# A four-layer transformer stack on one core: another order for the last chunks between the mixing layers and the expert layer

## The chip, the cores and the metric

The kernel runs on one core of a Trainium2 chip. The metric is the device time of one execution in microseconds (us), the median of three runs. The engines are TensorE (PE in the profile), VectorE (DVE), ScalarE (ACT), GpSimd (POOL) and SyncE (SP), which work from queues of their own and wait for one another by semaphores.

## The reference, cut to what matters

```python
x = x + layernorm(attention(layernorm(x)))                  # 32 x 256 rows of 128
x = x + layernorm(ffn(layernorm(x)))                        # gated hidden layer of 512, two gelu layers
x = x + layernorm(recurrence(layernorm(x)))                 # h = tanh(xt + h @ Wh.T + bh)
x = x + layernorm(experts(layernorm(x)))
def experts(x):
    shared_out = (silu(x @ sg) * (x @ su)) @ sd
    logits = x @ gate_w                                     # 32 experts
    expert = argmax(logits);  score = sigmoid(max(logits))
    xs = (x * score)[argsort(expert)]                       # rows sorted by expert
    routed = (silu(xs @ g[e]) * (xs @ u[e])) @ d[e]
    return shared_out + routed[inverse order]
```

All is float32 with 8192 rows of 128 numbers. The recurrence runs over the 256 positions of all 32 sequences at once. A chunk of 512 rows holds 16 positions, that is 16 steps of 32 columns, and the state goes on from chunk to chunk.

## The kernel before, in words

After an attention stage the rows go through the mixing stage in 16 chunks of 512 rows (numbers 0 to 15). Each chunk passes a pipeline of rounds: first norm and the feed-forward layers (PE lines 1371 to 1451), third norm and the recurrence, the shared part of the expert layer, routing, and a scatter of its rows into the DRAM tensor `sorted_d`, in which each expert owns pages of 128 rows. After the last full round a function called `drain` in each engine's program finishes the chunks that are still in the pipe. It is called with n2, n1, n0 = 13, 14, 15, and chunk 12 is left to scatter. Then the slot stage reads `sorted_d` in pairs of pages, runs the routed experts (PE lines 1529, 1543, 1551, 1558) and writes the output by indirect DMAs from POOL.

The change touches `drain` alone, with the helpers that it calls. Every engine executes its own list in order, so the lists are the schedule. What they hold for one chunk:

- DVE: `sums` and `residual` (line 1755, 1738, 1766), `recurrence_norm` (1738, writes `xn3`), `choose` (1782 to 1793, top expert and one-hot), `shared(q, m)` (1746, 1750, the two halves m = 0, 1 of the shared expert's hidden layer `shid`), `state_stats` (1729, 1733), `gated` (1800 to 1810, the gated row, owner and row number into `row_buf`), `third_sum` (1738, 1870, `hs` and the sum into `row_buf`, then its statistics), `third_norm` (1738, writes `xn4`), `turn_pages` (1821 to 1838, page bookkeeping, 14 small operations) and `place` (1853 to 1860, the row positions `pos_i`).
- POOL: `rstd` (1212, 1214), the root behind each norm, and `scatter` (1223), four indirect DMAs that need `pos`, `rows` and `sh_out` of their chunk.
- ACT: the tanh of each recurrence step (1578), copies out of PSUM (`recurrence_turned` 1594, `router_turned` 1590, `shared_out` 1598, `state_turned` 1608), the gate's tanh (1603) and the shared part's tanh (1584).
- PE: `turn4` (1279, transposes), `recurrence_in` (1333), `rnn` (1286, one recurrence step), `logits` (1316), `ranks` (1340 to 1345), `shared` (1311), `shared_down` (1324), `state_turn` (1356) and `keep_busy` (1351), products that nobody reads.

A recurrence step is a round trip: PE's small product adds into `xi`, ACT's tanh writes `state`, and the next product waits for it. The 16 steps of chunk 15 lie in the drain with nothing else of the pipeline beside them.

There are two row buffers: even chunks use `row_buf[0]`, odd ones `row_buf[1]`, and `third_sum` waits until the buffer's former chunk has been scattered:

```python
apply("h", hs, lambda k: hs[:, k, :], "hn", h)
wait(dve, s[f"placed{side}"], 8 * CT * (h - side))
dve.tensor_tensor(third, hs[:], old[:], ALU.add).then_inc(s["x3"], 1)
```

SP issues the loads of the experts' weights (`wgu`, `wd`, 2 MB each DMA) as soon as the last product of chunk 15's feed-forward layer is done. They run on the same 16 DMA engines as the scatters.

## Time and profile before

| | |
|---|---|
| runs | 1768.71, 1770.89, 1771.26 us; median 1770.89 |
| the profiled execution, its own time | 1770.72 us |
| its span | 1769.0 us |
| PE busy | 1650.8 us (93%) |
| DVE busy | 1317.2 us (74%) |
| ACT busy | 889.0 us (50%) |
| POOL busy | 1000.8 us (57%) |
| last product of the feed-forward layers ends | about 1492.2 us |
| first transpose of the slot stage starts | 1566.25 us |

Times in the trace count from the span's start. The drain is the stretch from about 1492 to 1566 us, and the slot stage fills the rest. Busy time of PE is counted from records whose ends are modelled, so a PE that shows as busy can still be short of its peak. The granted clock is given as a share of 2.4 GHz: 1.00 or 0.50, and a value between is a stretch that has both.

### The profile page before, as it was taken

The page shows a single profiled execution, that of the slowest core. Times are in us where ns is not written, and L with a number is a line of the kernel's source. Part 1 is how long each engine was busy: PE and PEld are TensorE (multiplying, and loading weights), DVE is VectorE, ACT ScalarE, POOL GpSimd, SP SyncE. Part 2 cuts the span into 40 slices and gives each one's busy share as a digit, 9 for nine tenths or more (in the row PEclk, how much of TensorE's full clock was granted, in tenths as well). Part 3 has the DMA queues.
Part 4 walks back from the last instruction along what each step waited for, and adds up shares of the span by engine and source line. Part 5 has one row for each costly group of instructions (what it writes and reads, how often), then busy time and mean ns, then how long its engine had stood idle before and what let it go on. Part 6 is the DMA issues. An engine that isn't in the chain of part 4 may idle for free.

```text
span 1769.0 us, 47120 instructions
## 1 busy us (share of the span) xinstructions
PE 1650.8 (93%) x14871; PEld 1237.2 (70%) x14871; DVE 1317.2 (74%) x3869; ACT 889.0 (50%) x2003; POOL 1000.8 (57%) x1782
## 2 busy tenths in 40 slices
PE   5999999999999999849999999999999999789996
PEld 3677777777777777537788888777787886555553
DVE  5588888888888888745567777777777775748886
ACT  2666666666666666514444444444444442224443
POOL 7788888888888888712223333333333333227777
PEclk9999999999999999969999999999999999689998
DMA  1011111111111113010110000000000002434441
GB/s 42 11 50 55 51 49 50 50 49 51 53 54 54 54 54 104 14 36 25 60 60 31 31 31 31 22 30 23 28 30 29 25 25 99 155 116 134 134 131 41
DMA packets 78259, 95.96 MB, mean 54 GB/s; under 512 B 7046, under 2 KB 62995, under 8 KB 78160
## 3 DMA queue, kind: packets, MB, share of 16 engines
q1 hardware_dynamic: 70992, 77.91, 13.9%
q0 software_dynamic: 7168, 16.87, 2.7%
q8 instruction: 46, 0.75, 0.2%
q14 instruction: 53, 0.43, 0.1%
HBM read 53.14 MB, written 43.69 MB: 55 GB/s over the span
## 4 chain that ended last, share of the span: by engine, by line
PE 39%; DVE 8%; issue 5%; POOL 2%; DMA 1%; ACT 1%; DVEq 0%; POOLq 0%; SPq 0%; ACTq 0%
PE main L1371 6%; PE main L1373 5%; PE main L1380 5%; PE main L1529 3%; PE yp L1451 3%; PE main L1311 2%; PE xi L1286 2%; PE main L1435 2%; PE main L1324 2%; PE main L1438 1%; PE main L1436 1%; PE route L1543 1%; PE xi L1543 1%; PE turn L1279 1%; POOL out L1269 1%
## 5 line engine op out<-in xcount | busy, mean ns | idle before, releaser
L662 ACT ACTIVATE wgu<-score 128x384 f32<-128x384 f32 x512 | 223.2, 490 | 80.2 <-PE score L484 78.8
L1371 PE MATMUL main<-hT_high,h_high 128*128 128x512 f32 x512 | 221.2, 432 | 0.9 <-ACT hT_high L1628 0.9
L1373 PE MATMUL main<-hT_high,h_low 128*128 128x512 f32 x512 | 201.3, 393 | 0.0
L506 PE MATMUL outp<-wgu 128*32 128x256 f32 (+1 forms) x4096 | 196.3, 333 | 3.3 <-POOL wgu L327 2.2
L327 POOL TENSOR_SCALAR_AFFINE_SELECT wgu<-wgu 128x512 f32<-128x512 f32 x256 | 166.4, 655 | 52.0 <-ACT wgu L662 34.3
L506 PEld LDWEIGHTS outp<-wgu 128*32 128x32 f32 x4096 | 116.6, 111 | 69.5 <-issue 23.3
L1380 PE MATMUL main<-hT_low,h_high 128*128 128x512 f32 x512 | 138.3, 391 | 0.1
L1936 DVE SCALAR_TENSOR_TENSOR th<-th,main 128x512 f32<-128x512 f32 x64 | 43.9, 685 | 115.2 <-ACT th L1655 115.2
L544 PE MATMUL back<-wout,wgu 128*128 128x128 f32 x1024 | 128.6, 280 | 0.0
L544 PEld LDWEIGHTS back<-wout,wgu 128*128 128x128 f32 x1024 | 121.8, 195 | 0.4
L1269 POOL DMA_INDIRECT out<-res,idx x96 | 96.7, 1008 | 44.3 <-issue 40.7
L1286 PEld LDWEIGHTS xi<-state,wh_sb 128*128 128x128 f32 x512 | 93.2, 195 | 38.4 <-ACT state L1578 22.3
L1578 ACT ACTIVATE state<-xi,bias 128x32 f32<-128x32 f32 x256 | 73.0, 285 | 85.5 <-PE xi L1286 83.8
L1380 PEld LDWEIGHTS main<-hT_low,h_high 128*128 128x128 f32 x512 | 96.1, 188 | 21.9 <-DVE hT_low L1890 0.8
L514 PE MATMUL total<-wgu,pick 128*32 128x256 f32 (+1 forms) x2048 | 108.2, 329 | 0.0
L1212 POOL TENSOR_SCALAR bve_f<-bmv_f 128x4 f32<-128x4 f32 x16 | 7.7, 483 | 175.9 <-DVE bmv_f L1733 175.9
L1371 PEld LDWEIGHTS main<-hT_high,h_high 128*128 128x128 f32 x512 | 97.0, 189 | 13.6 <-ACT hT_high L1628 1.4
L1619 ACT ACTIVATE hT_high<-main,sc 128x512 fp32r<-128x512 f32 x64 | 44.0, 687 | 124.1 <-PE main L1380 124.1
L1207 POOL TENSOR_TENSOR hT_low<-wgu,hT_high 128x512 fp32r<-128x512 f32 x64 | 82.7, 1292 | 41.3 <-ACT wgu L1620 41.0
L1373 PEld LDWEIGHTS main<-hT_high,h_low 128*128 128x128 f32 x512 | 97.1, 190 | 11.7 <-issue 0.2
L1529 PE MATMUL main<-wgu,xgT 128*128 x192 | 101.6, 612 | 3.4 <-DVE hid_g L1989 2.4
L680 ACT ACTIVATE wgu<-back 128x512 f32<-128x512 f32 x128 | 76.4, 597 | 51.4 <-PE back L559 48.1
(295 smaller groups left out, 4361.4 us busy)
## 6 DMA issues: line engine op xcount, KB each, us to landing
sorted_d<-row_buf SPq DMA_DIRECT2D x26, 772.0 KB, 3.7
xg<-sorted_d SPq DMA_DIRECT2D x48, 386.0 KB
wgu<-in_gate_up SPq DMA_DIRECT2D x4, 2048.0 KB
xa<-in_x SPq DMA_DIRECT2D x32, 128.0 KB, 3.4
xr<-in_x SPq DMA_DIRECT2D x32, 128.0 KB, 3.2
x_d<-x SPq DMA_DIRECT2D x32, 128.0 KB, 1.8
x1c<-x_d SPq DMA_DIRECT2D x16, 256.0 KB, 2.8
x1v<-x_d SPq DMA_DIRECT2D x16, 256.0 KB, 2.7
```

The costliest lines, as they stand in the source:

```text
L327: pool.affine_select(out=blocks, in_=blocks, compare_op=ALU.is_ge, fill=0.0, base=0, pattern=[[0, 4], [1, P]], channel_multiplier=-1).then ...
L506: m = pe.matmul(outp[AUG * j:AUG * (j + 1), p % 2, k * P:T], val[par][:, k, h, v:v + AUG], weights(h, k), start=(k == 0), stop=(k == 1), t ...
L514: m = pe.matmul(total[AUG * j:AUG * (j + 1), k * P:T], pick[:, g, :], weights(GH * g + j, k), start=(g == 0 and k == 0), stop=(g == GROUPS ...
L544: m = pe.matmul(back[:, i * P:(i + 1) * P], onT[1 - par][:, c, i * P:(i + 1) * P], wout[:, c, :], start=(c == 0 and i == 0), stop=(c == PA ...
L662: act.activation(prob[:, h // 2 % (RING // 2), :, h % 2, :], score[h % BANKS][:, 0:SC].rearrange("p (c q) -> p c q", q=P), ACT.Exp).then_i ...
L1207: pool.tensor_tensor(hT_part[1][1][:, m, :], hT[1][:, m, :], hT_part[1][0][:, m, :].bitcast(F32), ALU.subtract).then_inc(s["h2_low"], 1)
L1269: pool.indirect_dma_start(out=out_rows[:, :], out_offset=bass.IndirectOffsetOnAxis(ap=idx[k][:, n:n + 1], axis=0), in_=res[k][:, n, :], in ...
L1286: pe.matmul(xi[:, o:o + B], wh_sb[:], state[:, prev:prev + B], start=False, stop=(t == STEPS - 1), skip_group_check=True).then_inc(s["p_st ...
L1371: pe.matmul(main[m % 2][:, :], w[0][:, k, m * P:(m + 1) * P], src[0][:, k, :], start=(k == 0), stop=False)
L1373: pe.matmul(main[m % 2][:, :], w[1][:, k, m * P:(m + 1) * P], src[0][:, k, :], start=False, stop=False)
L1380: mm = pe.matmul(main[m % 2][:, :], w[0][:, k, m * P:(m + 1) * P], src[1][:, k, :], start=False, stop=(k == HC - 1))
L1529: pe.matmul(main[2 * (r % 2) + i][:, :], xgT[r % 2][:, i * P:(i + 1) * P], wgu[:, bass.ds(e, 1), :].rearrange("p o i -> p (o i)"), start=T ...
```

## The change

In `drain` of each engine, and nowhere else (line numbers behind the change are higher by 7 to 9 in the DVE part):

- POOL scatters chunk 12 before the roots of chunk 15's norms, and chunk 13 only after all roots.
- A third row buffer holds chunk 15 (`rows=2`), so that neither its `gated` nor its `third_sum` waits for the scatter of chunk 13. `place` of chunk 15 now waits for that scatter, since it writes the same `pos_i`.
- DVE makes the choice of chunk 13 before `recurrence_norm`, and does `state_stats`, `gated`, `third_sum` and `third_norm` of chunk 15 ahead of `turn_pages` and `place` of chunk 14.
- PE puts behind 10 of the 16 recurrence steps two products without a reader (`keep_busy(1)`, 512 columns, and one of 128 columns), moves `ranks` of chunk 14 behind the last step, and has other counts of `keep_busy`: 3 for 5, 2 new ones, 20 for 10, 8 for 4. `turn4` of chunk 15 stands before `shared_down` of chunk 14.
- ACT runs `gate` of chunk 14 behind `state_turned`, and the transposed copy of chunk 15 before `shared_out` of chunk 14.

```diff
 POOL
             def drain(n2, n1, n0):
+                scatter(n2 - 1, n2 % 2, 0, CT)
                 rstd("y", n0)
                 rstd("x", n0)
-                scatter(n2 - 1, n2 % 2, 0, CT)
                 rstd("h", n1)
                 rstd("e", n1)
-                scatter(n2, n1 % 2, 0, CT)
                 rstd("h", n0)
                 rstd("e", n0)
+                scatter(n2, n1 % 2, 0, CT)
                 scatter(n1, n0 % 2, 0, CT)
-                scatter(n0, n1 % 2, 0, CT)
+                scatter(n0, n1 % 2, 0, CT, 2)
 PE
+                def rnn_busy(n, bank):
+                    for _ in range(n):
+                        rnn()
+                        keep_busy(1, bank)
+                        pe.matmul(bank[:, 0:P], w1_part[0][:, 0:P], w1_part[0][:, 0:P], start=True, stop=True)
...
-                keep_busy(5, turn)
+                keep_busy(3, turn)
                 wait(pe, s["xn3"], n0 + 1)
                 turn4(xn3[:], "p_xn3T")
                 recurrence_in(n0)
                 rnn()
                 ranks(n2, route)
-                rnn(5)
+                rnn_busy(6, turn)
+                keep_busy(2, turn)
                 shared_down(n2, rnn)
                 rnn()
                 wait(pe, s["xn4"], n1 + 1)
                 wait(pe, s["xn3T"], n0 + 1)
                 turn4(xn4[:], "p_xn4T")
-                rnn(2)
+                rnn_busy(2, main[3])
                 wait(pe, s["y"], n0 + 1)
                 logits(n1, yp)
-                rnn(3)
-                ranks(n1, yp)
+                rnn_busy(2, main[3])
                 rnn(STEPS)
                 wait(pe, s["xn4T"], n1 + 1)
                 state_turn(n0)
+                ranks(n1, yp)
                 wait(pe, s["sh_out"], n2 + 1)
                 shared(n1, 0)
                 shared(n1, 1, 0)
-                keep_busy(10, xi)
-                shared_down(n1, lambda: None)
+                keep_busy(20, xi)
                 wait(pe, s["xn4"], n0 + 1)
                 wait(pe, s["hs"], n0 + 1)
                 turn4(xn4[:], "p_xn4T")
+                shared_down(n1, lambda: None)
                 wait(pe, s["pos"], n2 + 1)
                 logits(n0, route)
                 wait(pe, s["sh_out"], n1 + 1)
                 shared(n0, 0)
+                shared(n0, 1, 0)
                 ranks(n0, route)
-                shared(n0, 1, 0)
-                keep_busy(4, xi)
+                keep_busy(8, xi)
                 shared_down(n0, lambda: None)
                 keep_busy(36, xi)
 ACT
-                rnn(8)
+                rnn(9)
                 shared_out(n2, n2 % 2)
                 rnn()
                 router_turned(n1)
-                rnn(5)
-                gate(n1)
                 rnn(STEPS)
                 state_turned(n0)
+                gate(n1)
                 shared(n1, 0)
                 shared(n1, 1, 0)
+                router_turned(n0)
                 shared_out(n1, n1 % 2)
-                router_turned(n0)
 DVE
                 residual(n0, o)
+                choose(n2, route)
                 recurrence_norm(n0, o)
                 shared(n2, 0)
-                choose(n2, route)
...
                 choose(n1, yp)
+                state_stats(n0)
                 gated(n1, e)
+                third_sum(n0, o, 2)
+                shared(n1, 0)
+                third_norm(n0, 2)
+                shared(n1, 1, 0)
                 turn_pages(n1, e, yp)
-                state_stats(n0)
-                shared(n1, 0)
-                third_sum(n0, o)
-                shared(n1, 1, 0)
-                third_norm(n0, o)
                 place(n1, e, yp)
                 choose(n0, route)
-                gated(n0, o)
+                gated(n0, 2)
                 shared(n0, 0)
                 shared(n0, 1, 0)
                 turn_pages(n0, o, route)
+                wait(dve, s[f"placed{o}"], 8 * CT * (n0 - o))
                 place(n0, o, route)
```

The order on PE, at the recurrence steps behind `ranks` of chunk 13 (`w_high` is the left operand of the products without a reader), as a piece of the difference:

```order
 L1342 MATMUL route<-onehot,before 128x32
 L1345 MATMUL route<-onehot,ones 128x32 x4
-L1286 MATMUL xi<-state,wh_sb 128x32 x5
+L1286 MATMUL xi<-state,wh_sb 128x32
+L1351 MATMUL turn<-w_high 128x512
+L1470 MATMUL turn<-w_high 128x128
+L1286 MATMUL xi<-state,wh_sb 128x32
```

Five steps in a row became six steps, each with a product of 512 and one of 128 columns behind it; four later steps have the same.

The order on DVE, behind the choice of chunk 14, before:

```order
L1793 TENSOR_TENSOR onehot<-rtop,first 128x128
L1800 TENSOR_SCALAR gate_val<-tanh_top 128x4
L1804 TENSOR_SCALAR row_buf<-xn,gate_val 128x128 x4
L1805 TENSOR_SCALAR row_buf<-first 128x4
L1807 CAST row_buf<-rid 128x4
L1810 TENSOR_SCALAR rid<-rid 128x4
L1821 TENSOR_TENSOR counts<-counts,yp 128x32
```

and behind the change:

```order
L1800 TENSOR_TENSOR onehot<-rtop,first 128x128
L1736 BN_STATS bstat_h<-hs 128x6 x4
L1740 BN_AGGR bmv_h<-bstat_h 128x2 x4
L1807 TENSOR_SCALAR gate_val<-tanh_top 128x4
L1811 TENSOR_SCALAR row_buf<-xn,gate_val 128x128 x4
L1812 TENSOR_SCALAR row_buf<-first 128x4
L1814 CAST row_buf<-rid 128x4
L1817 TENSOR_SCALAR rid<-rid 128x4
L1745 TENSOR_SCALAR hs<-hs,bmv_h,brs_h 128x128 x4
L1878 TENSOR_TENSOR row_buf<-hs,x 128x4x128
```

The statistics of chunk 15's state and its sum now stand before the page operations of chunk 14, which came right behind `gated`.

The order on POOL, at the scatter of chunk 13, before:

```order
L1223 DMA sorted_d<-row_buf,pos_i 13312x386 x4
L1212 TENSOR_SCALAR bve_h<-bmv_h 128x4
L1214 TENSOR_TENSOR brs_h<-bve_h,pow_half 128x4
L1212 TENSOR_SCALAR bve_e<-bmv_e 128x4
L1214 TENSOR_TENSOR brs_e<-bve_e,pow_half 128x4
L1223 DMA sorted_d<-row_buf,pos_i 13312x386 x8
```

and behind the change:

```order
L1212 TENSOR_SCALAR bve_h<-bmv_h 128x4
L1214 TENSOR_TENSOR brs_h<-bve_h,pow_half 128x4
L1212 TENSOR_SCALAR bve_e<-bmv_e 128x4
L1214 TENSOR_TENSOR brs_e<-bve_e,pow_half 128x4
L1223 DMA sorted_d<-row_buf,pos_i 13312x386 x12
```

The scatter of chunk 13 left its place ahead of chunk 15's last two roots and stands with those of 14 and 15 at the end.

## Rows read from the trace of the kernel before

**Rows 1.** Windows: stretch and busy us of each engine, granted clock, DMA share, GB/s

```profile
1495.00:1500.00 5.00, 5.00 (x13) 2.93 (x13) 3.06 (x13) 0.60 (x1) 1.63 (x3) 0.51 1.04 376
...
1505.00:1510.00 5.00, 3.46 (x26) 2.41 (x26) 3.14 (x19) 1.96 (x7) 1.62 (x3) 0.88 1.04 381
1510.00:1515.00 5.00, 1.03 (x4) 0.90 (x5) 3.52 (x13) 0.29 (x1) 1.20 (x2) 0.50 1.06 298
...
1530.00:1535.00 5.00, 5.00 (x11) 2.32 (x11) 4.48 (x21) 1.19 (x2) 1.23 (x2) 0.73 0.00 0
```

**Rows 2.** Timeline of PE in the drain: start us, us, what, idle before and releaser

```profile
1493.38 0.63 PE L1279 MATMUL turn<-ident,xn 128*128 128x128 f32 x4 [0.78 <-ACT hs L1608]
...
1504.99 1.13 PE L1333 MATMUL xi<-xn3T,wi_sb 128*128 128x512 f32 x2 [0.69 <-ACT xn3T L1594]
...
1508.21 0.41 PE L1286 MATMUL xi<-state,wh_sb 128*128 128x32 f32 x2 [0.38 <-ACT state L1578]
1509.00 0.64 PE L1286 MATMUL xi<-state,wh_sb 128*128 128x32 f32 x2 [0.38 <-ACT state L1578]
1510.01 0.64 PE L1286 MATMUL xi<-state,wh_sb 128*128 128x32 f32 x2 [0.38 <-ACT state L1578]
1514.60 1.22 PE L1324 MATMUL main<-sd,shid 128*128 128x128 f32 x4 [3.96 <-DVE shid L1750]
...
1522.15 1.89 PE L1316 MATMUL yp<-gate_sb,xn4T 128*128 128x32 f32 x8
...
1527.98 1.09 PE L1356 MATMUL turn<-ident,state 128*128 128x128 f32 x4 [0.47 <-ACT state L1578]
1528.86 5.49 PE L1311 MATMUL main<-xn4T,sgu 128*128 128x512 f32 x8
...
1552.98 8.42 PE L1351 MATMUL xi<-w_high 128*128 128x512 f32 x36
```

**Rows 3.** Timeline of ACT, the copy of chunk 15's state

```profile
1529.11 0.60 ACT L1608 ACTIVATE hs<-turn 128x512 f32<-128x512 f32 x1 [1.27 <-PE turn L1356]
```

**Rows 4.** Timeline of DVE in the drain

```profile
1500.33 1.14 DVE L1738 TENSOR_SCALAR xn<-x,bmv_x,brs_x 128x128 f32<-128x128 f32 x4 [1.48 <-POOL brs_x L1214]
...
1502.91 0.28 DVE L1782 TENSOR_REDUCE top<-route 128x4 f32<-128x128 f32 x1
...
1504.52 0.87 DVE L1729 BATCH_NORM_STATS2 bstat_h<-hs 128x6 f32<-128x128 f32 x4
...
1511.17 0.69 DVE L1870 TENSOR_TENSOR row_buf<-hs,x 128x512 f32<-128x512 f32 x1 [2.73 <-DMA sorted_d<-row_buf,pos_i]
1511.89 0.87 DVE L1729 BATCH_NORM_STATS2 bstat_e<-row_buf 128x6 f32<-128x128 f32 x4
...
1513.10 0.66 DVE L1746 SCALAR_TENSOR_TENSOR th<-th,main 128x512 f32<-128x512 f32 x1
...
1514.69 1.11 DVE L1738 TENSOR_SCALAR xn<-row_buf,bmv_e,brs_e 128x128 f32<-128x128 f32 x4
1515.84 0.19 DVE L1821 TENSOR_TENSOR counts<-counts,route 128x32 f32<-128x32 f32 x1
...
1520.98 0.17 DVE L1860 CAST pos_i<-pos 128x4 int32<-128x4 f32 x1
...
1531.91 0.87 DVE L1729 BATCH_NORM_STATS2 bstat_h<-hs 128x6 f32<-128x128 f32 x4
...
1545.21 0.29 DVE L1782 TENSOR_REDUCE top<-route 128x4 f32<-128x128 f32 x1 [2.63 <-PE route L1316]
...
1556.17 0.17 DVE L1860 CAST pos_i<-pos 128x4 int32<-128x4 f32 x1
```

**Rows 5.** Chain that ended last, at the scatter of chunk 12: start us, us, what

```profile
1504.30 6.77 DMA sorted_d<-row_buf,pos_i
```

**Rows 6.** Timeline of POOL in the drain

```profile
1494.37 0.19 POOL L1212 TENSOR_SCALAR bve_y<-bmv_y 128x4 f32<-128x4 f32 x1 [15.80 <-DVE bmv_y L1733]
...
1560.41 0.96 POOL L1223 DMA_INDIRECT sorted_d<-row_buf,pos_i  x1 [0.30 <-issue]
```

More of the change, by code:

```diff
@@ L1214, in rstd, with scatter @@
                 pool.tensor_tensor(rs[n][:], ve[n][:], pow_half[:], ALU.pow).then_inc(s["rs" + n], 1)
-            def scatter(z, par, k0, k1):
+            def scatter(z, par, k0, k1, rows=None):
                 if z is None:
@@ L1223, in scatter @@
                     pool.indirect_dma_start(out=sorted_d[:, :], out_offset=bass.IndirectOffsetOnAxis(
-                        ap=pos_i[par][:, k:k + 1], axis=0), in_=row_buf[1 - par][:, k, :], in_offset=None)\
+                        ap=pos_i[par][:, k:k + 1], axis=0), in_=row_buf[1 - par if rows is None else rows][:, k, :], in_offset=None)\
                         .then_inc(s[f"placed{1 - par}"], 16)
@@ L1696, in drain @@
                 shared(n0, 1, 0)
-                shared_out(n0, n0 % 2)
+                shared_out(n0, 2)
             rounds(act, step, drain)
@@ L1864, in state_stats, with third_sum @@
                 stats("h", lambda k: hs[:, k, :], h)
-            def third_sum(h, side):
-                third, old = row_buf[side][:, :, THIRD:THIRD + D], x2[side]
+            def third_sum(h, side, rows=None):
+                third, old = row_buf[side if rows is None else rows][:, :, THIRD:THIRD + D], x2[side]
                 apply("h", hs, lambda k: hs[:, k, :], "hn", h)
-                wait(dve, s[f"placed{side}"], 8 * CT * (h - side))
+                if rows is None:
+                    wait(dve, s[f"placed{side}"], 8 * CT * (h - side))
                 dve.tensor_tensor(third, hs[:], old[:], ALU.add).then_inc(s["x3"], 1)
@@ L2037, in build @@
         wgu = sb("wgu", [P, E, 2 * I])
-        row_buf = [sb(f"row_buf{i}", [P, CT, ROW]) for i in range(2)]
+        row_buf = [sb(f"row_buf{i}", [P, CT, ROW]) for i in range(3)]
         with ExitStack() as early:
```

## The prediction

> **What bounds the kernel now.** Only the drain changes, so I read it from its end backwards. The chain that ended last runs there through DVE for most of its length, then through the four scatter DMAs of chunk 15 on POOL, and from them into the slot stage. DVE starts the choice of chunk 15 at 1545.21, has its positions at 1556.34 [rows 4], and POOL issues the last of the four at 1560.41 [rows 6]. The slot stage cannot begin before this scatter has landed, and it is left as it is. So what counts is how much earlier that choice of chunk 15 can begin.
>
> The timeline of DVE shows what held it up before. First it stood 2.73 us in front of the sum of chunk 14 [rows 4], waiting for the scatter of chunk 12, whose last DMA took 6.77 us [rows 5] while the expert weights filled all DMA engines (their share is 1.04 to 1.06) [rows 1]. Then it did the page work of chunk 14 ahead of the statistics of chunk 15's state, which started at 1531.91 [rows 4], though ACT had the state at 1529.71 [rows 3]. The timeline of PE shows why the state itself is late. A step costs 0.79 us at the granted clock 1.00 (1508.21 to 1509.00) and 1.01 us at 0.50 (1509.00 to 1510.01). The clock fell at about 1509 while PE did nothing but single steps with waits of 0.38 us, and then `shared_down` of chunk 13 stood 3.96 us [rows 2], for the half of `shid` that DVE computes behind that same sum of chunk 14. At 0.50 everything from 1510 to beyond 1530 was done [rows 1].
>
> **Part 1: scatter of chunk 12 first, third buffer.** POOL stood idle for 15.80 us up to 1494.37, when it could have issued that scatter; four issues take 4 x (0.96 + 0.30) = 5.0 us [rows 6], so they fit. The price of the move is nothing as long as that idle stretch covers it; without it, 5.0 us would stand in front of chunk 15's first root. The DMAs are now issued before the weight loads, and DVE's 2.73 us vanish. The scatter of chunk 13 moves behind the last roots, so POOL issues 12 DMAs in a row at the end. Those of 13 (5.0 us) come behind chunk 15's last root, about 1529, and have landed before `place` of chunk 15, near 1545, which now waits for them. Those of 14 take until about 1542. POOL is then free when chunk 15 has its positions. Cost 0; cover 3 us and more.
>
> **Part 2: the choice of chunk 13 before the third norm.** It takes 1.61 us (1502.91 to 1504.52) [rows 4] and now lies in DVE's wait for the root of that norm, which is 1.48 us long [rows 4]. That delays the norm by 0.1 us, which PE does not see, as it is busy until 1503. Everything behind it on DVE comes 1.6 us earlier. With the 2.73 us, the sum of chunk 14 is 4.2 us earlier, so `shid` of chunk 13 is ready at 1514.60 - 4.2 = 1510.4.
>
> **Part 3: the recurrence on PE.** One filler product of 512 columns takes 0.234 us (8.42 us for 36) [rows 2]. Two fewer of them before the third transposes bring the recurrence's input from 1504.99 to 1504.5. The second filler, of 128 columns, has no row; it costs at least 0 and at most what the product of four times its width does, 0.234. A pair thus takes 0.23 to 0.47 us, in a gap of 0.38 [rows 2]. Since part of the step's own 0.41 us is pipeline too, I take no delay; the upper end costs 0.09 x 10 = 0.9 us. At the clock 1.00 the fourth step comes at 1507.7, the seventh at 1507.7 + 3 x 0.79 = 1510.1, and behind its pair and the two extra fillers (0.5 us) `shared_down` of chunk 13 starts at 1511.0 instead of 1514.60. From there 9 steps remain: 0.65 us to the first, 8 x 0.79 = 6.3, `logits` of chunk 14 between them 0.9 (half of 1.89, as it ran at half clock) [rows 2], ACT's two copies between steps 0.3, and 0.75 for the last round trip. The state's transposes start at 1519.9 instead of 1527.98 [rows 2], and at twice the clock they are 0.5 us shorter. The state is there at 1529.71 - 8.1 - 0.5 = 1521.1.
>
> **Part 4: DVE from the state on.** DVE has done the choice of chunk 14 by then (logits at 1517.6, choice until 1519.2), so it waits for the state: this wait takes the place of the old ones. Then, with rows [rows 4]: statistics and root 2.75 us (as 1511.89 to 1514.69, 2.80, for the next norm; `gated` of chunk 14, seven small operations, hides in it), norm 1.15 (1514.69 to 1515.84), sum 0.72, statistics and root 2.80 with `shared(14, 0)` inside, norm 1.15, `shared(14, 1)` 1.45 (1513.10 to 1514.55, the end that releases `shared_down`), pages and positions of chunk 14 5.35 (1515.84 to 1521.15 and a gap). The sum is 15.4 us, so the choice of chunk 15 starts at 1521.1 + 15.4 = 1536.5, not 1545.21: **8.7 us earlier**. The tail of 11.1 us behind it has the same operations.
>
> **Part 5: the other queues.** PE, from 1520.4: `ranks` 0.4, `shared` of chunk 14 at full clock about 3.5 (5.49 with most of it at half clock) [rows 2], 20 fillers 4.7, until 1529.0. Chunk 15's norm gives `xn4` at 1521.1 + 8.6 = 1529.7, so the fillers end 0.7 us in time. Its logits are there near 1534.3, 2 us before DVE wants them. ACT's `gate` of chunk 14 stands behind the state's copy, and still ahead of `gated`. The 8 fillers for 4 end in the time in which DVE does chunk 15's shared part. The last 36 and the gap to the slot stage keep their distance from the final positions. SP's list is unchanged, and its weight loads end by about 1522, long before the slots.
>
> **The sum.** The profiled execution took 1770.72 us (span 1769.0). 1770.72 - 8.7 = 1762.0 us. That execution lies 0.2 us under the median of 1770.89, so the median should move by as much. A measurement of this kernel tells a change from none at about 0.2%, 3.5 us: below 1767.3 is faster, above 1774.4 slower.
>
> **The rivals.** *A, the forecast*: the clock stays at 1.00 through the steps. For it: after the fall at about 1495 PE worked through 5 us without a pause, the clock came back, and then it stayed up until about 1509, through single steps with nothing in their gaps (0.88 over 1505 to 1510, PE busy 3.46 of 5 us) [rows 1]. A step with its pair leaves hardly a gap. 1762.0, own range 1759.0 to 1764.5.
>
> *B, the clock falls in the second half of the steps*, from 1515 on, where only four steps have fillers and the rest is transposes, small logits and waits for ACT. It was at 0.51 over 1495 to 1500 [rows 1], and ahead of that fall PE had done little but two sets of transposes and logits, with waits of 0.78 us between [rows 2]. Five steps at 1.01 cost 1.1 us more, logits 0.9, transposes 0.5, and fillers now as long as their gap about 1.1: 3.6 us back, 1765.6. The Trainium skill, page TensorE: Matmul & The Clock Gate, section Part 4: PE-mode transpose, says that transposes do not count as activity for the clock gate in the way matmuls do. By that rule the stretch around the two sets of transposes is the one at risk, and B is likelier than A's count of busy time says; no row here separates transposes from the waits beside them.
>
> *C, the clock falls at about 1509 as before*, since the products in the gaps are too little. The fourth step is at 1507.7; then steps at 1.01 to 1.2, fillers of 0.47, `shared_down` with 1.28 us a piece as before, and the last ten steps take until about 1526.5. The state is there 7 us later than in A. 1762.0 + 7 = 1769.0, within 0.2% of before.
>
> *D, slower*: the fillers themselves pace PE. They stand in PE's queue ahead of each step. At half clock a pair costs up to 0.94 us, a step with it 0.64 + 0.94 = 1.58. Ten of these, the two single fillers and `shared_down` at half clock give the state at about 1532.4. It decides from 1545.2 - 15.4 = 1529.8: a later state makes the kernel slower. Here by 2.6 us, and if the 20 fillers also run at half clock (9.4 us, in front of chunk 15's transposes, behind 6.8 us of `shared`) the choice comes at about 1556, 11 us late: 1773 to 1782, middle 1777. Against it: PE's clock rose again within 4 us of the same `shared` products before (0.73 over 1530 to 1535) [rows 1].
>
> *E, another wait takes the rest*: DVE or POOL wait in an order that I have not seen, for instance `place` of chunk 15 for the scatter of chunk 13. Half of the gain goes: 1766, up to 1769.
>
> **How the numbers follow.** A 0.57, B 0.17, C 0.11, D 0.05, E 0.10. B, A and most of E are faster by over 0.2%, C and a part of E within it. That gives faster 0.81, same 0.14, slower 0.05. The range takes A's lower end (tail and slot stage start at another moment of the clock, 1 us, and steps a little faster than 0.79 with `logits` hidden, 2 us) and reaches up to C: 1759.0 to 1768.5.
>
> **What would show it.** Right: a granted clock of 1.00 from 1502 to the end of the drain, steps 0.79 us apart with the fillers between, no wait for the scatter's DMA on DVE, `shared_down` of chunk 13 near 1511, the state's copy near 1520.5, the choice of chunk 15 near 1536.5, the first scatter of chunk 15 near 1548, the slot stage's first transposes near 1557.5. Wrong: 0.50 between 1509 and 1525 (C, D), steps over 1.2 us apart (D), DVE or POOL waiting in front of `place` or the last scatter (E), or a slot stage that itself takes longer than the 203 us from 1566.25 to the span's end.

## The result, and the profile of the changed kernel

The changed kernel took 1758.34 us, median of 6 runs (1752.7 to 1759.53), against 1769.78 us (1767.92 to 1771.26, 6 runs) of the kernel before in the same comparison. The ratio is 0.9930 with an interval of 0.9915 to 0.9945: faster by 0.7%, 11.4 us. I had forecast 1762.0 us in a range of 1759.0 to 1768.5. The direction was right, and the time lies 0.7 us under the range.

The profiled execution took 1755.85 us with a span of 1754.1 us, 14.9 us less than the span of before. I cut both spans at the same three events: the first DVE operation on `y` of chunk 15, where the drain begins, the first transposes of the slot stage, and the end.

| stretch, us | before | changed | difference |
|---|---|---|---|
| start to the drain | 1492.28 | 1488.58 | 3.70 |
| drain | 73.97 | 64.53 | 9.44 |
| slot stage | 202.75 | 200.99 | 1.76 |
| span | 1769.0 | 1754.1 | 14.9 |

The first row holds no changed instruction. The first copy of the attention stage (`y_sb`, on ACT) stands at 83.65 us before and at 79.45 us here, so a difference of 4.2 us is there by then, of which 3.70 are left at the drain. The second row is the one that I had forecast, at 8.7 us.

PE's timeline of the changed kernel, at the steps, the shared part and the start of the slots (start us, us, what, idle before and releaser):

```profile
1499.22 1.13 PE L1333 MATMUL xi<-xn3T,wi_sb 128*128 128x512 f32 x2 [0.69 <-ACT xn3T L1601]
...
1501.65 0.41 PE L1286 MATMUL xi<-state,wh_sb 128*128 128x32 f32 x2
1501.90 0.48 PE L1351 MATMUL turn<-w_high 128*128 128x512 f32 x1
1502.22 0.22 PE L1470 MATMUL turn<-w_high 128*128 128x128 f32 x1
1502.44 0.41 PE L1286 MATMUL xi<-state,wh_sb 128*128 128x32 f32 x2
...
1506.59 0.71 PE L1324 MATMUL main<-sd,shid 128*128 128x128 f32 x4 [0.49 <-DVE shid L1757]
...
1511.82 1.03 PE L1316 MATMUL yp<-gate_sb,xn4T 128*128 128x32 f32 x8
...
1515.11 0.63 PE L1356 MATMUL turn<-ident,state 128*128 128x128 f32 x4 [0.47 <-ACT state L1585]
...
1519.04 5.12 PE L1351 MATMUL xi<-w_high 128*128 128x512 f32 x20
1525.26 0.66 PE L1279 MATMUL turn<-ident,xn 128*128 128x128 f32 x4 [1.09 <-DVE xn L1745]
...
1553.11 0.66 PE L1565 MATMUL turn<-ident,xg 128*128 128x128 f32 x2 [4.82 <-DMA xg<-sorted_d]
```

Against [rows 2], counted from the start of the drain: the recurrence's input comes at 10.6 us, not 12.7, `shared_down` of chunk 13 at 18.0, not 22.3, and with a wait of 0.49 us, not 3.96. The state's transposes come at 26.5, not 35.7. A step with its two products without a reader takes 0.79 us (1501.65 to 1502.44), as a step alone did in the kernel before at the granted clock 1.00.

Windows of the changed kernel (stretch, busy us of each engine with instructions, granted clock, DMA share, GB/s), beside [rows 1], where 1510 to 1515 had 0.50:

```profile
1500.00:1505.00 5.00, 4.93 (x39) 3.35 (x37) 4.64 (x25) 2.21 (x7) 1.26 (x2) 1.00 1.06 322
1505.00:1510.00 5.00, 4.51 (x33) 3.90 (x33) 4.41 (x19) 1.57 (x5) 1.20 (x2) 1.00 1.06 290
1510.00:1515.00 5.00, 4.49 (x29) 3.31 (x27) 4.13 (x17) 2.29 (x8) 0.00 (x0) 1.00 1.05 290
...
1550.00:1555.00 5.00, 1.28 (x3) 0.79 (x4) 0.42 (x1) 0.00 (x0) 0.00 (x0) 0.55 0.76 246
```

The timeline of ACT has the state's copy, 13.3 us earlier than [rows 3], and 9.6 us earlier when both are counted from the drain's start:

```profile
1515.77 0.60 ACT L1616 ACTIVATE hs<-turn 128x512 f32<-128x512 f32 x1 [0.81 <-PE turn L1356]
```

On DVE's timeline the sum of chunk 14 (1503.16) has no wait in front, where [rows 4] show 2.73 us for the scatter, and the one long wait that is left is the one for the state, 1.83 us. Positions of chunk 15 come 11.1 us after its choice, as before:

```profile
1496.71 1.12 DVE L1745 TENSOR_SCALAR xn<-x,bmv_x,brs_x 128x128 f32<-128x128 f32 x4
...
1503.16 0.69 DVE L1878 TENSOR_TENSOR row_buf<-hs,x 128x512 f32<-128x512 f32 x1
...
1516.47 1.06 DVE L1736 BATCH_NORM_STATS2 bstat_h<-hs 128x6 f32<-128x128 f32 x4 [1.83 <-ACT hs L1616]
...
1532.10 0.29 DVE L1789 TENSOR_REDUCE top<-route 128x4 f32<-128x128 f32 x1
...
1543.04 0.17 DVE L1867 CAST pos_i<-pos 128x4 int32<-128x4 f32 x1
```

On POOL's timeline the scatter of chunk 12 ends 6.79 us ahead of the first root, and those of 13, 14 and 15 stand behind the last one:

```profile
1479.03 1.05 POOL L1223 DMA_INDIRECT sorted_d<-row_buf,pos_i  x1 [4.12 <-DVE pos_i L1867]
...
1490.68 0.19 POOL L1212 TENSOR_SCALAR bve_y<-bmv_y 128x4 f32<-128x4 f32 x1 [6.79 <-DVE bmv_y L1740]
...
1524.13 1.05 POOL L1223 DMA_INDIRECT sorted_d<-row_buf,pos_i  x1 [0.18 <-issue]
...
1532.47 0.96 POOL L1223 DMA_INDIRECT sorted_d<-row_buf,pos_i  x1 [3.47 <-DVE pos_i L1867]
...
1543.49 0.96 POOL L1223 DMA_INDIRECT sorted_d<-row_buf,pos_i  x1 [6.27 <-DVE pos_i L1867]
```

### The profile page after: what moved, and what is told of

It reads as the page before. It is cut to its first block, busy times and chain, and to the rows that moved or that the text cites. A ratio compares the mean times of both kernels' runs of the same rounds, so it can differ in the third digit from the quotient of the medians.

```text
span 1754.1 us, 47186 instructions
## 1 busy us (share of the span) xinstructions
PE 1642.4 (94%) x14905; PEld 1229.3 (70%) x14905; DVE 1317.4 (75%) x3869; ACT 888.7 (51%) x2003; POOL 1000.0 (57%) x1782
## 4 chain that ended last, share of the span: by engine, by line
PE 40%; DVE 8%; issue 4%; POOL 2%; ACT 1%; DMA 0%; DVEq 0%; POOLq 0%; SPq 0%; ACTq 0%
PE main L1371 6%; PE main L1373 5%; PE main L1380 5%; PE main L1536 3%; PE yp L1451 3%; PE xi L1286 2%; PE main L1311 2%; PE main L1435 2%; PE main L1324 2%; PE main L1438 1%; PE main L1436 1%; PE route L1550 1%; PE xi L1550 1%; POOL out L1269 1%; PE turn L1279 1%
```

## The experiments

All twelve compute the whole reference. For each I give the time and the length of the drain in its one profile: from DVE's first `y` operation of chunk 15 to the first slot transposes, 73.97 us before and 64.53 us changed. "Over the changed kernel" means over 1757.9 us, its median in all its 11 executions of this study.

**The changed kernel again.** Only a blank line is added.

```diff
+
```

> The changed kernel once more, unchanged. Profiles so far put the start of the drain anywhere from 1488.0 to 1492.3 us whatever the kernel, and the drain itself at 64.5 us. Theory 1 (the gain is the drain's 8.7 to 9.5 us, and what went beyond came from the head of those runs): ratio to before 0.9945 to 0.995, a median 8.5 to 10 us under before. Theory 2 (the change gains more than its drain shows): 12 us again.

1757.35 us (1756.24 to 1759.99, 5 runs) against 1767.66 (16 runs), ratio 0.9938 (0.9925 to 0.9950): 10.3 us. The drain took 64.48 us, 0.05 from the first time, but it began at 1491.52, not 1488.58, and the first copy of the attention stage came 4.30 us later. The slot stage took 202.20 us, not 200.99. ACT's timeline in the first profile of the changed kernel, and in this one:

```profile
79.45 0.38 ACT L734 ACTIVATE y_sb<-back 128x256 f32<-128x256 f32 x1 [0.37 <-PE back L544]
```

```profile
83.75 0.38 ACT L734 ACTIVATE y_sb<-back 128x256 f32<-128x256 f32 x1 [0.37 <-PE back L544]
```

So the same program has its first copy 4.3 us later in one execution than in another, and reaches the drain 2.9 us later. The 3.70 us in front of the drain are of that size, and the kernel of the next experiment, which has the program of before, reaches its drain at 1487.95, earlier than either: they are chance. The granted clock differs between the two profiles in this stretch (0.50 over 25 to 28 and 35 to 41 us in the first, 1.00 in both windows and 0.50 over 59 to 65 us in this one). That this makes the difference isn't shown.

Over all comparisons of this study the kernel before has a median of 1767.9 us (60 runs, 1763.7 to 1771.4) and the changed one 1757.9 (11 runs): 10.0 us, of which the drain is 9.4.

**The third buffer alone**, in the kernel before, unused.

```diff
-        row_buf = [sb(f"row_buf{i}", [P, CT, ROW]) for i in range(2)]
+        row_buf = [sb(f"row_buf{i}", [P, CT, ROW]) for i in range(3)]
```

> The kernel before with a third row buffer that is allocated and used by nobody; the program is otherwise that of before. Theory 1 (the gain lies in the drain, and the head of the changed kernel's profile was 3.7 us early by chance): same time as before, within 2 us, and in its profile the first chunk of y at the drain (DVE line 1755) between 1488 and 1493. Theory 2 (the shifted addresses make the stages ahead of the drain faster): 3 to 4 us under before, and that product near 1488.5. The drain itself lasts 74 us from there to the slot stage's first transposes in both.

1766.19 us (12 runs), ratio 0.9994 (0.9984 to 1.0004): no difference. The other addresses explain nothing. Its drain took 75.64 us, 1.7 more than the 73.97 of before with the same list. The state was there 1.6 us earlier (35.8 us into the drain for 37.4), but from the choice of chunk 15 to its positions it took 13.0 us for 11.1. PE did the shared part of chunk 15 at half clock here:

```profile
1540.00:1545.00 5.00, 5.00 (x22) 2.59 (x23) 4.04 (x15) 0.80 (x2) 2.76 (x3) 0.50 0.42 158
```

In the profile of before that stretch had 1.00. So the drain of the old list has a spread of its own, and against this profile the changed drain is 11.1 us shorter, not 9.4.

**The scatter of chunk 12 first, and nothing else**, in the kernel before.

```diff
             def drain(n2, n1, n0):
+                scatter(n2 - 1, n2 % 2, 0, CT)
                 rstd("y", n0)
                 rstd("x", n0)
-                scatter(n2 - 1, n2 % 2, 0, CT)
```

> The kernel before with one edit: chunk 12 is scattered ahead of the roots of chunk 15's first norms. Theory 1 (the wait of 2.73 us in front of the sum of chunk 14 feeds shared_down of chunk 13, and with it the recurrence): the wait is gone, the time is 2.5 to 3 us under before. Rival (DVE and PE find another wait in its place, since the page work of chunk 14 stands in front of the state's statistics): under 1 us gained.

1765.55 us (12 runs, 1760.92 to 1767.68), ratio 0.9986 (0.9975 to 0.9997): 2.5 us. DVE's 2.73 us for the scatter are gone. Its drain took 67.86 us, 6.1 less than before, which is more than the time shows. The profiled execution (1761.4 us) lies at the low end of these 12 runs, so I take the time and not the drain as the size. Why this list varies by 7 us between executions stays open; the kernel before did so by 7.7 us in 60 runs.

**The reverse: the changed kernel with that scatter back behind two roots.**

```diff
-                scatter(n2 - 1, n2 % 2, 0, CT)
                 rstd("y", n0)
                 rstd("x", n0)
+                scatter(n2 - 1, n2 % 2, 0, CT)
```

> The changed kernel with the scatter of chunk 12 back behind the roots of chunk 15's first two norms. Theory 1 (its last DMA lands beside the weight loads, and the wait of about 2.7 us in front of the sum of chunk 14 comes back, and is passed on through shid, shared_down and the steps): the state 2.7 to 4 us later than in the changed kernel, 2.5 to 4 us slower. Rival (with DVE's choice moved and the fillers in place that wait is covered): under 1 us slower.

1764.11 us (11 runs), ratio 0.9979 (0.9967 to 0.9991), and a drain of 71.23: 6.2 us over the changed kernel by the pooled time, 6.7 by the drain. I had expected 2.5 to 4. DVE's timeline, PE's and the windows show how one wait grows:

```profile
1507.78 0.69 DVE L1878 TENSOR_TENSOR row_buf<-hs,x 128x512 f32<-128x512 f32 x1 [3.46 <-DMA sorted_d<-row_buf,pos_i]
```

```profile
1511.21 1.22 PE L1324 MATMUL main<-sd,shid 128*128 128x128 f32 x4 [4.95 <-DVE shid L1757]
...
1521.93 0.63 PE L1356 MATMUL turn<-ident,state 128*128 128x128 f32 x4 [0.47 <-ACT state L1585]
```

```profile
1505.00:1510.00 5.00, 1.26 (x6) 0.78 (x6) 2.15 (x10) 0.29 (x1) 0.12 (x1) 0.99 1.04 320
1510.00:1515.00 5.00, 3.79 (x18) 3.79 (x18) 4.34 (x18) 0.57 (x2) 1.08 (x2) 0.50 1.05 290
```

DVE waits 3.46 us, PE then 4.95 us in front of `shared_down`. The clock is at 0.50 when this idle time ends, a piece of `shared_down` takes 1.22 us for 0.71, and the state's transposes come at 33.1 us after the drain's start for 26.5. Of these 6.6 us, 4.4 are there when `shared_down` starts (22.4 for 18.0), and 2.2 come at half clock behind it. The steps here have their pairs, and in the changed kernel, which differs by this scatter alone, the clock stayed up: filled steps did not keep it up when PE stood idle behind them.

**The changed kernel with PE's and ACT's lists of before** (the reverse of those parts of the diff, entire).

```diff
-                keep_busy(3, turn)
+                keep_busy(5, turn)
...
-                rnn_busy(6, turn)
-                keep_busy(2, turn)
+                rnn(5)
...
-                keep_busy(20, xi)
+                keep_busy(10, xi)
+                shared_down(n1, lambda: None)
```

> The changed kernel with the lists of PE and ACT as before; DVE, POOL and the third buffer as changed. Theory 1 (PE's list gives the early state, and without it DVE only waits longer): the state is ready about 32 to 33 us after y, the choice of chunk 15 starts 15.6 us later, at 48 to 49; 4 to 6 us slower than the changed kernel, and no better than the kernel before with the early scatter alone (46.8). Rival (the early scatter and DVE's order carry the gain): within 2 us of the changed kernel.

1763.51 us (11 runs), ratio 0.9975 (0.9965 to 0.9986), drain 68.84: 5.6 us over the changed kernel. Its windows and DVE's timeline:

```profile
1505.00:1510.00 5.00, 3.16 (x14) 2.75 (x14) 4.59 (x17) 1.00 (x4) 1.20 (x2) 0.50 1.06 292
1510.00:1515.00 5.00, 4.90 (x24) 4.67 (x23) 4.26 (x19) 1.90 (x6) 0.00 (x0) 0.52 1.05 290
```

```profile
1521.97 1.06 DVE L1736 BATCH_NORM_STATS2 bstat_h<-hs 128x6 f32<-128x128 f32 x4 [3.61 <-ACT hs L1615]
```

The state is ready at 31.6 us into the drain for 27.8, and DVE waits 3.61 us for it, not 1.83. So PE's and ACT's lists are worth more than half of the gain. Undone alone, they cost 5.6 us and the early scatter 6.2, together more than the 10.0 that both kernels differ by: the two parts need each other, and their prices don't add up. `shared_down` starts at 18.0 us here as in the changed kernel, and all four of its pieces then take about 1.2 us, at half clock.

**The pair of products behind the steps left out.**

```diff
                     for _ in range(n):
                         rnn()
-                        keep_busy(1, bank)
-                        pe.matmul(bank[:, 0:P], w1_part[0][:, 0:P], w1_part[0][:, 0:P], start=True, stop=True)
```

> The changed kernel without the two products behind ten of the recurrence steps (two single keep_busy stay). Theory 1 (these products hold the clock at 1.00 while the steps run): the clock falls to 0.50 within the steps, the state is ready 5 to 7 us later than in the changed kernel, the time is 1763 to 1766. Rival (the clock falls only after some 7 us of steps and the earlier shared_down breaks that stretch, so the order alone keeps it up): 1758 to 1759, granted clock 1.00 over the steps.

1756.55 us (1754.56 to 1761.3, 6 runs), ratio 0.9937 (0.9921 to 0.9952): no slower than the changed kernel, and the expectation of my own theory was missed. Its drain is 65.94, 1.4 longer. The windows and the timeline of PE:

```profile
1505.00:1510.00 5.00, 3.48 (x12) 2.79 (x13) 4.50 (x17) 1.44 (x5) 1.47 (x3) 0.57 1.06 295
1510.00:1515.00 5.00, 4.87 (x30) 4.50 (x29) 4.42 (x21) 1.77 (x6) 0.00 (x0) 0.75 1.05 289
1515.00:1520.00 5.00, 3.40 (x22) 2.98 (x23) 2.75 (x10) 1.81 (x6) 0.00 (x0) 0.94 0.86 237
1520.00:1525.00 5.00, 5.00 (x25) 2.56 (x23) 3.62 (x20) 1.80 (x4) 1.26 (x2) 0.72 0.02 5
```

```profile
1505.73 0.63 PE L1286 MATMUL xi<-state,wh_sb 128*128 128x32 f32 x2 [0.38 <-ACT state L1583]
1506.75 0.63 PE L1286 MATMUL xi<-state,wh_sb 128*128 128x32 f32 x2 [0.38 <-ACT state L1583]
...
1511.36 1.20 PE L1324 MATMUL main<-sd,shid 128*128 128x128 f32 x4
...
1512.58 0.69 PE L1324 MATMUL main<-sd,shid 128*128 128x128 f32 x4
```

The clock does fall, as I had said: steps are 1.02 us apart from 1505.73 on. But `shared_down` starts only 0.3 us later, since the steps ahead of it had slack towards `shid`. The clock is back at 1.00 for its third piece, where in the kernel before it stayed at 0.50 beyond 1530 [rows 1]. The fall costs 1.3 us of the state in this profile, not the 7 us of my case C.

**All products without a reader left out but the last 36.** Beside the pairs, `keep_busy(3)`, `(2)`, `(20)` and `(8)` go.

```diff
-                        keep_busy(1, bank)
-                        pe.matmul(bank[:, 0:P], w1_part[0][:, 0:P], w1_part[0][:, 0:P], start=True, stop=True)
...
-                keep_busy(3, turn)
...
-                keep_busy(2, turn)
...
-                keep_busy(20, xi)
...
-                keep_busy(8, xi)
```

> The changed kernel without any product without a reader in the drain, but for the last 36. Theory 1 (with the work this close together the clock matters little as long as DVE is the bound: the state comes 1 to 2 us later, and half clock in logits and shared of chunk 15 takes more than PE's 2 us of slack): 2 to 5 us slower than the changed kernel. Rival (they are needed throughout): 8 us or more slower, back to before. Second rival (they buy nothing): the same time.

1761.25 us (6 runs), ratio 0.9964 (0.9949 to 0.9978), drain 67.33: 3.4 us over the changed kernel. The drain has 2.8 of them. Some 0.6 us lie outside the profiled span: the time is at least 2.35 us longer than the span in five of these six runs, and 1.7 to 1.8 us longer in the runs of every other kernel of this study. I have no reason for that. With the run before, the pairs are worth 0 to 1.4 us and the other 33 products the rest, 1.4 us of drain at least.

The clock fell during the steps in this profile too, but it came back later than in the run before. `shared_down` ran wholly at half clock, and the state came 2.8 us late, not 1.3:

```profile
1505.00:1510.00 5.00, 3.31 (x14) 2.84 (x13) 4.62 (x17) 1.15 (x4) 1.20 (x2) 0.50 1.05 292
1510.00:1515.00 5.00, 5.00 (x25) 4.91 (x25) 4.35 (x20) 1.70 (x6) 0.00 (x0) 0.50 1.04 288
```

**DVE's middle order of before**, in the changed kernel (page work of chunk 14 ahead of chunk 15's sum; `ranks` and `gate` moved so that it finds its inputs).

```diff
-                state_stats(n0)
                 gated(n1, e)
-                third_sum(n0, o, 2)
+                turn_pages(n1, e, yp)
+                state_stats(n0)
                 shared(n1, 0)
-                third_norm(n0, 2)
+                third_sum(n0, o, 2)
                 shared(n1, 1, 0)
-                turn_pages(n1, e, yp)
+                third_norm(n0, 2)
```

> The changed kernel with DVE's old order behind the choice of chunk 14 (its page work ahead of the statistics of chunk 15's state), and ranks and gate of chunk 14 ahead of the last recurrence step, as before. Theory 1 (DVE is saturated once the state is there, so its order is worth nothing as such, and the 1.8 us in which it waits for the state could hold page work): the same time as the changed kernel or up to 1.5 us less; the choice of chunk 15 starts 42 to 43.5 us after y. Rival (the order is a part of the gain, as the page work of 3.2 us no longer stands in front of the state): 1.5 to 3 us slower.

1757.36 us (5 runs), ratio 0.9939 (0.9926 to 0.9952), drain 63.73: the same time, the drain 0.8 us shorter. In the changed kernel DVE waits 1.83 us for the state, and page work that fills this wait costs nothing. No run here shows a gain from the new order of DVE alone.

**Two buffers in the changed kernel.** Chunk 15 uses the odd buffer, and the scatter of chunk 13 goes ahead of chunk 15's last two roots.

```diff
+                scatter(n2, n1 % 2, 0, CT)
                 rstd("h", n0)
                 rstd("e", n0)
-                scatter(n2, n1 % 2, 0, CT)
                 scatter(n1, n0 % 2, 0, CT)
-                scatter(n0, n1 % 2, 0, CT, 2)
+                scatter(n0, n1 % 2, 0, CT)
...
-                third_sum(n0, o, 2)
+                third_sum(n0, o)
```

> The changed kernel with two row buffers: chunk 15 uses the odd one again, chunk 13 is scattered before the roots of chunk 15's state, and third_sum waits for it. Theory 1 (what delayed the drain before was the scatter of chunk 12 beside the weight loads, not the number of buffers): 0 to 1.5 us slower than the changed kernel, a wait of under 1 us for the scatter of chunk 13. Rival (the third buffer carries a good part of the gain): 3 us or more slower, with a wait of that length in front of the sum of chunk 15.

1759.04 us (6 runs), ratio 0.9952 (0.9938 to 0.9967), drain 64.68, against 64.53. DVE does not wait for the scatter, only 0.43 us more for the root behind it:

```profile
1521.65 1.12 DVE L1745 TENSOR_SCALAR hs<-hs,bmv_h,brs_h 128x128 f32<-128x128 f32 x4 [0.58 <-POOL brs_h L1214]
```

The third buffer with the late scatter is worth 0.15 us in the drain and about 1 us in the time, which 6 runs can't tell from nothing.

**Two more steps ahead of `shared_down`.** PE waits 0.49 us there, and DVE 1.83 us for the state.

```diff
-                rnn_busy(6, turn)
-                keep_busy(2, turn)
+                rnn_busy(8, turn)
                 shared_down(n2, rnn)
...
-                rnn_busy(2, main[3])
+                rnn_busy(1, main[3])
...
-                rnn(9)
+                rnn(11)
```

> The changed kernel with eight instead of six recurrence steps (each with its two products) ahead of shared_down of chunk 13, where PE waits 0.5 us for shid behind two single keep_busy, which go. Theory 1 (from y to the state the chain of 16 steps is the bound, then DVE is): the state is there 1.2 to 1.6 us earlier, DVE's wait of 1.8 us in front of its statistics is nearly gone, the drain shrinks from 64.5 us to 63 to 63.5. Rival (what stands behind moves by as much, the logits of chunk 14 among it, so DVE only waits elsewhere): drain 64 to 65 us.

1757.23 us (5 runs), ratio 0.9943 (0.9929 to 0.9956), drain 63.28. DVE's wait for the state goes from 1.83 to 0.43 us, and the drain is 1.25 us shorter. The time alone can't show 1.25 us in 5 runs.

```profile
1512.36 1.06 DVE L1735 BATCH_NORM_STATS2 bstat_h<-hs 128x6 f32<-128x128 f32 x4 [0.43 <-ACT hs L1615]
```

**54 for 36 products at the end.** PE is idle for 4.82 us ahead of the slots, and the window from 1550 has a granted clock of 0.55.

```diff
-                keep_busy(36, xi)
+                keep_busy(54, xi)
```

> The changed kernel with 54 instead of 36 products without a reader at the drain's end, so that they fill PE's 4.8 us of idling in front of the slot stage. Theory 1 (the clock falls to 0.50 in that gap in every profile and the first slots run slowly for 3 to 7 us): the granted clock stays 1.00, the slot stage takes 199 to 200.5 us from its first transposes to the end, instead of 201 to 202.7; 1 to 2.5 us faster in the time. Rival (the start of the slot stage waits for its loads and copies, not for PE's clock): stage at 201 to 202 us and the same time.

1755.07 us (1752.38 to 1756.7, 5 runs), ratio 0.9926 (0.9911 to 0.9942). The drain is 64.61, unchanged, and the slot stage takes 199.36 us, where it took 200.82 to 202.75 in the twelve profiles with 36 products. The time is 2.8 us under the changed kernel's, a little more than I had expected (1 to 2.5). Its windows, and PE's timeline:

```profile
1550.00:1555.00 5.00, 3.53 (x17) 2.48 (x15) 0.42 (x1) 0.00 (x0) 0.00 (x0) 1.00 0.59 179
1555.00:1560.00 5.00, 5.00 (x20) 2.74 (x21) 2.03 (x5) 1.83 (x5) 0.00 (x0) 1.00 1.02 354
```

```profile
1553.94 0.41 PE L1565 MATMUL turn<-ident,xg 128*128 128x128 f32 x2 [0.86 <-DMA xg<-sorted_d]
```

**Both of these together.**

```diff
-                rnn_busy(6, turn)
-                keep_busy(2, turn)
+                rnn_busy(8, turn)
...
-                rnn_busy(2, main[3])
+                rnn_busy(1, main[3])
...
-                keep_busy(36, xi)
+                keep_busy(54, xi)
...
-                rnn(9)
+                rnn(11)
```

> Both edits, eight steps first and 54 products at the end. Theory 1: the two gains add up, 2 to 4 us under the changed kernel, 1753.5 to 1755.5. Rival: neither shows in the time, 1757 to 1758.

1752.18 us (1750.94 to 1753.55, 5 runs), ratio 0.9915 (0.9902 to 0.9929), drain 63.27 and slots 199.40 us. In the profile they add up: the drain is that of the first edit (63.28), the slot stage that of the second (199.36). Drain and slot stage of this profile together are 2.9 to 4.0 us shorter than in the two profiles of the changed kernel. The time is 5.7 us under the changed kernel's, more than the 2 to 4 that I had expected, and what is beyond the two pieces is not explained. This version beats both kernels: 15.3 us under its kernel before, where the changed kernel in the same manner was 10.3 under.

## Why the prediction was right in its direction and off in its size

**Part 1, right.** The four issues of chunk 12 stood in POOL's idle time with 6.8 us to spare, DVE's wait is gone, the scatters of 13 and 14 were over before `place` of 15 could wait. Case E did not happen. By the two runs the move is worth 2.5 us of time in the old lists (its one profile has the drain 6.1 us shorter) and 6 us in the new ones. In the new ones it is a condition: without it PE idles 4.95 us at `shared_down`.

**Part 2, right.** The third norm (`xn`, 1496.71) has no wait in front of it; the choice lies in the time of the root.

**Part 3, mechanism right, state put 1.0 us too late.** Counted from the drain's start I had the recurrence's input at 12.2 us; it came at 10.64. Two fewer fillers gave 0.41 us, as forecast 0.5 (11.05 in the run with PE's old list). The other 1.66 us belonged to the one profile of before, whose clock was at 0.51 over 1495 to 1500 [rows 1]: 12.71 there, and 11.05 in each of three other kernels with the same list. The pairs cost nothing, as I took it: in the row of 1502.22 a product of 128 columns shows 0.22 us, of which 0.16 overlap with the product of 512 columns before it, and the step stays at 0.79 us. `shared_down` came at 18.0 for 18.7, waiting for `shid`, not behind the steps. The state's copy ended at 27.8 for 28.8.

**Part 4, right.** From the state's statistics to the choice of chunk 15 it took 15.63 us, forecast 15.4, the tail 11.1 as forecast. So the drain measured 64.53 us; my sum made it 73.97 - 8.7 = 65.3.

**Part 5, right but for the end.** The 20 fillers ended 1.09 us ahead of the transposes, forecast 0.7. The slot stage did not keep its length: 202.75 us before, 200.99 and 202.20 in the two profiles of the changed kernel. In all three PE's clock is low after the gap of 4.8 us, and it comes back at different moments: 7.4 us after the stage's first transposes before, 4.2 and 7.5 us after them in the changed kernel. The run with 54 products shows that about 2 us hang on this gap.

**The step that failed is the base of the sum, and with it the low end of the range.** I took 1770.72 us of one profiled execution, subtracted the drain's 8.7, and let everything outside the drain come again exactly. For A's lower end I gave 1 us to the slot stage's clock and 2 us to the steps, and nothing to the 1492 us in front of the drain. That base was 2.8 us above what became the median of 60 runs, 1767.9. The drain's term was 0.7 us too small (8.7 for 9.44). 1762.0 - 2.8 - 0.7 = 1758.5, and 1758.34 was measured. The stretch in front of the drain took 1485.69 to 1492.28 us in the fourteen profiles of this study, and the execution that I built on had the largest of these values. A range around 1767.9 - 8.7 = 1759.2 would have held the result. The mechanism of the drain stands. Of the 11.4 us measured, 10.0 are there in all the runs taken together, the rest being this spread. That the gain of the drain came out within 0.7 us has some luck in it: the old list's other profile has a drain of 75.64, not 73.97.

**Rivals B and C fell, and with them part of A's reason.** In both profiles of the changed kernel the clock stayed at 1.00 through the steps and up to the gap before the slots, as A says, but in the run without the pairs it fell three times from the steps to the slots, and that run was no slower. C's mechanism was there; its price of 7 us was taken from the kernel before, where the fall came with 3.96 us of idle time at `shared_down`. The fall made the state late by 1.3 us in the run without the pairs and by 2.8 us in the one that left out the other products too: the clock came back later there. The early `shid` counts for more than the pair: the run with the late scatter has the pairs, the idle time and the fall, its state is 6.6 us late, and it is 6 us slower. A fall such as B's, just behind the steps, shows in the run with DVE's old order, which has the pairs (0.50 over 1519 to 1522 us, behind the state's transposes at 1518.34). It came after the state and cost nothing that shows. The run with 54 products, which is the changed kernel up to the drain's last products, has another (0.50 over 1528 to 1530), and a drain of the same length to 0.1 us. The Trainium skill, page TensorE: Matmul & The Clock Gate, section Part 4: PE-mode transpose, would have made the stretch of the two sets of transposes the one at risk. The granted clock was 1.00 there with the pairs and 0.94 over 1515 to 1520 without them, so the trace doesn't decide on this rule: the fall in the run with DVE's old order would fit it, and no run changes the transposes alone. D, the pairs as the pace of PE, is excluded at the full clock by the 0.79 us a step. At half clock they never ran in any profile, so their price there is open.

**How the gain divides, when the parts are added in this order.** Scatter first: 2.5 us. The rest of POOL's list, DVE's order and the third buffer on top of it: about 2 us in time (1765.55 to 1763.51, intervals overlapping) and none in the drain of the profiles (67.86 and 68.84), so nothing that can be told. PE's and ACT's lists on top: 5.6 us. Without most of the products without a reader the kernel is 3.4 us slower, so these make 3.4 of it, and the order and the last products the rest. No run has the new products in the old order.

## What to carry to other kernels

Cut the span at events that both kernels share and put a spread on each piece from several executions before setting a range: here the edited 4% of the changed kernel repeated to 0.1 us in two profiles, that of the old list moved by 1.7, and the rest of the program by several us. A wait in front of an in-order engine can be worth more than its own length when another engine's queue stalls behind it and its clock falls in the stall: 3.46 us of DVE cost 6 in the new lists, while 2.73 us cost 2.5 of time in the old ones. Products without a reader pay in gaps of idle time ahead of heavy work (18 more at the end of the drain: 2 us), and hardly between short steps that have slack.

## What the runs showed of the hardware that I had not expected

- The price of a fall of the clock depends on when the clock comes back, and that moment moves between kernels that do nearly the same work. Without the pairs it fell at about 1505.7, in single steps with waits of 0.38 us and no longer gap, and was back for the third piece of `shared_down` (pieces of 1.20, then 0.69 us): 1.3 us. With the other products left out too, all of `shared_down` ran at 1.20 us a piece: 2.8 us. In the kernel before, the clock stayed low from about 1509 to beyond 1530 [rows 1].
- The slot stage's length goes with the time that the clock is at 0.50 behind its first transposes, in all fourteen profiles: 199.36 and 199.40 us with none, 200.82 with 3.4 us, 200.99 with 4.2, 201.43 with 5.7, 202.20 with 7.5, 202.75 with 7.4.
- A product of 128 columns adds about 0.06 us behind one of 512 columns: they end at 1502.22 + 0.22 and 1501.90 + 0.48. One of 512 in a row of its like adds 0.23 [rows 2]. The ends of products are modelled, so the 0.06 is an estimate.
- The scatter's last DMA of chunk 15 landed in 2.63 us when no weights were being loaded (the changed kernel's chain), and that of chunk 12 in 6.77 us beside the weight loads [rows 5].

```profile
1547.28 2.63 DMA sorted_d<-row_buf,pos_i
```

- The start of the program varies by 4.5 us (first copy of the attention stage at 79.45 to 83.95 us in fourteen profiles) though no run changes anything there. The stretch from that copy to the drain varies by about as much, 1405.7 to 1409.9 us, so the spread of the times has more than one source.
